# Router logits from unscaled rows with centred gate weights, and the routing's turns, ranks and logits spread over the slots

## The reference, cut

```python
def _ln_t(v, eps=1e-05):
    m = jnp.mean(v, axis=-1, keepdims=True)
    s = jnp.var(v, axis=-1, keepdims=True)
    return (v - m) / jnp.sqrt(s + eps)
...
x = x + _L1_conv_ref(_ln_c(x), ...)              # projections, spikes, attention, output projection
t = _to_tokens(x)
t = t + _L1_ffn_ref(_ln_t(t), ...)
...
def _L1_ffn_ref(x, Wg, bg, W1, b1, W2, b2):
    logits = jnp.einsum('bsd,de->bse', x, Wg) + bg
    topk_vals, topk_idx = jax.lax.top_k(logits, 2)
    topk_w = jax.nn.softmax(topk_vals, axis=-1)
    ...                                          # the two experts of each token, weighted
```

## Time and profile before

| what | us |
|---|---|
| median of 3 runs (1244.0 to 1249.71) | 1247.43 |
| profiled execution | 1248.21 |
| its span | 1246.2 |
| busy: PE / PEld / DVE / ACT / POOL | 980.1 / 822.9 / 828.8 / 625.8 / 550.9 |
| mean granted TensorE clock (share of full speed) | 0.872 |

### The profile page before, as it was taken

One profiled execution on the slowest core, in us unless ns is written; L12 is line 12 of the kernel. 1 busy time (PEld: TensorE's weight loads), 2 busy tenths in 40 slices (PEclk: granted clock), 3 DMA queues, 4 the chain that ended last, 5 costly groups with the idle time before them and its releaser, 6 DMA issues. The chain is left out here.

```text
span 1246.2 us, 23615 instructions
## 1 busy us (share of the span) xinstructions
PE 980.1 (79%) x6627; PEld 822.9 (66%) x6628; DVE 828.8 (67%) x2699; ACT 625.8 (50%) x1334; POOL 550.9 (44%) x707
## 2 busy tenths in 40 slices
PE   9958838767677676876777541499999999999997
PEld 7848825545456464664555530388888888888886
DVE  7724435746759889797885664266666666666665
ACT  3434413475597868778754530244444444444443
POOL 3310001012133566676665764355555554555454
PEclk9979969976778898788877555699999999999999
DMA  8668576900010010000000100111111111111110
GB/s 341 287 186 286 187 212 158 254 19 20 21 51 20 28 46 22 19 26 13 29 15 31 37 25 34 41 51 35 45 48 50 41 48 52 48 41 47 49 40 2
DMA packets 83331, 93.56 MB, mean 75 GB/s; under 512 B 7709, under 2 KB 75549, under 8 KB 79930
## 3 DMA queue, kind: packets, MB, share of 16 engines
q1 hardware_dynamic: 74201, 75.33, 20.5%
q0 software_dynamic: 9056, 17.33, 4.2%
HBM read 56.07 MB, written 38.32 MB: 76 GB/s over the span
## 5 line engine op out<-in xcount | busy, mean ns | idle before, releaser
L1838 POOL DMA_INDIRECT out_dram<-res,index x155 | 154.9, 999 | 216.3 <-DVE res L1904 187.8
L1947 ACT ACTIVATE sil<-ps_h 128x512 f32<-128x512 f32 x155 | 92.6, 597 | 253.0 <-PE ps_h L1999 253.0
L1869 DVE TENSOR_TENSOR act_rows<-ps_h,sil 128x512 f32<-128x512 f32 x155 | 107.2, 692 | 132.3 <-ACT sil L1947 132.3
L2018 PE MATMUL ps_y<-r_raw,aT 128*128 x1240 | 163.8, 275 | 0.0
L159 POOL DMA_INDIRECT slots<-x_sb,r_pos x128 | 129.4, 1011 | 48.3 <-issue 37.3
L2018 PEld LDWEIGHTS ps_y<-r_raw,aT 128*128 128x128 f32 x1240 | 150.7, 192 | 0.1
L1997 PE MATMUL ps_h<-r_raw,uTh 128*128 x310 | 136.6, 441 | 1.6 <-DVE uTl L1863 1.6
L1998 PE MATMUL ps_h<-r_raw,uTh 128*128 x310 | 123.7, 399 | 0.0
L1999 PE MATMUL ps_h<-r_raw,uTl 128*128 x310 | 122.1, 394 | 0.0
L1089 PE MATMUL ps_q<-wqkv,zT 128*128 128x256 f32 x256 | 113.0, 533 | 0.0
L1089 PE MATMUL ps_q<-zT,wqkv 128*128 128x128 f32 x256 | 71.3, 371 | 33.9 <-DVE ps_q L1057 18.3
(11 more groups left out here) (257 smaller groups left out, 2361.9 us busy)
## 6 DMA issues: line engine op xcount, KB each, us to landing
wc<-in_mixing_weights SPq DMA_DIRECT2D x8, 2048.0 KB, 14.8
slots<-zero SPq DMA_DIRECT2D x4, 2652.0 KB, 23.2
pay<-slots SPq DMA_DIRECT2D x39, 272.0 KB, 2.9
x_sb<-in_token_rows SPq DMA_DIRECT2D x8, 1088.0 KB, 6.8
sblk<-coefficients SPq DMA_DIRECT2D x16, 256.0 KB, 6.1
mixed<-mo SPq DMA_DIRECT2D x16, 256.0 KB, 8.2
gin<-mixed SPq DMA_DIRECT2D x16, 256.0 KB, 14.2
r_raw<-in_L_ffn_W SPq DMA_DIRECT2D x8, 508.0 KB
```

The source lines that it names most:

```text
L1838: nc.gpsimd.indirect_dma_start(out_rows, bass.IndirectOffsetOnAxis(at, 0), res[:, m % RES, :], None, bounds_check=TOKENS - 1, oob_is_err=F ...
L1869: nc.vector.tensor_tensor(act_rows[:, k], ps_h[:, k, :, DFF:], sil[:, k], ALU.mult).then_inc(s_act, 1)
L1947: nc.scalar.activation(sil[:, k], ps_h[:, k, :, 0:DFF], ACT.Silu).then_inc(s_sil, 1)
L2018: ins = nc.tensor.matmul(dst, aT[:, k, (2 * e + h) * P:(2 * e + h + 1) * P], raw[:, 4 + h, col], start=(h == 0), stop=(h == 1))
```

## The change

The rows are no longer scaled before the turn. A row's normalised value is (row - mean) times the inverse deviation, so the logits are the inverse deviation times the raw row times gate weights from which the mean over channels is taken off, plus the bias. The centred weights `wg_c` are made once on PE with a matrix `centre` (identity less 1/128). `route_rows` and the buffer `r_y` go; the choice multiplies by the deviation first and so has 16 links.

The order changes with it. On PE a new function `between` stands between `project_out` and `project`: there come the ranks (slot 1 instead of 0), the turns of z in slots 0 to 2, one routing turn in each of slots 3 to 6, and a quarter of the logits in each of slots 4 to 7. On ACT a new function `ahead` stands before the projection's sign: `major`, parts of `u_rows` and `x_rows`, the copies `rT`, and the third group of `z_rows` in slot 7. In pass 0 both kinds stay behind. On DVE the start of the placing moves from slot 0 to 1, its second part from 1 to 2, the deviation from 2 to 3, and two statistics rows stand alone in slot 0. In the tail block 6's turns and logits come in slots 1 and 2, its choice in slot 3, ranks in slot 4, placing in slots 5 and 6; block 7's logits are interleaved with its turns, and the folding of weights comes after block 7's choice.

```diff
         def route_choose(dve, v, rows=None, limit=0):
             dve.wait_ge(s_lg, v + 1)
+            dve.wait_ge(s_rn, v + 1)
             need(dve, s_paid, v)
-            chain.link(nc.vector.tensor_tensor(lg[:, :, :], logits_bank(v).rearrange("p (q e) -> p q e", e=E),
-                                               bg[:, :].unsqueeze(1).broadcast_to([P, NT, E]), ALU.add))
+            by_tile = lambda x: x.rearrange("p (b j) e -> p b j e", j=2)
+            chain.link(nc.vector.tensor_tensor(by_tile(lg[:, :, :]), by_tile(logits_bank(v).rearrange("p (q e) -> p q e", e=E)),
+                                               payload(SCALE, v).unsqueeze(3).broadcast_to([P, B, 2, E]), ALU.mult))
+            chain.link(nc.vector.tensor_tensor(lg[:, :, :], lg[:, :, :], bg[:, :].unsqueeze(1).broadcast_to([P, NT, E]), ALU.add))
...
         def route_turn(pe, v, g):
-            pe.wait_ge(s_ry, v * G + g + 1)
-            if v == NP2 - 1 and g < 2:
+            pe.wait_ge(s_x, (v + 1) * B)
+            if v == NP2 - 2 and g < 2:
                 pe.wait_ge(s_sq, NP2 * B)
+            elif v == NP2 - 1 and g < 2:
+                pe.wait_ge(s_rz, v * G - 2 + g + 1)
...
-        def route_logits(pe, v):
-            pe.wait_ge(s_rz, v * G + 4)
+        def route_logits(pe, v, g0=0, g1=G):
+            pe.wait_ge(s_rz, v * G + g1)
...
             @block.vector, beside(i, b)
-                    if b == 0 and r >= 1:
-                        route_start(dve, r - 1, output_done[r], NT - 2)
+                    if b == 0 and r >= 0:
+                        output_done[r].upto(NT - 2)
+                    if b == 1 and r >= 1:
+                        route_start(dve, r - 1)
                     if b == 1 and r >= 0:
                         route_stats(dve, r, output_done[r])
-                    if b == 1 and r >= 1:
+                    if b == 2 and r >= 1:
                         route_turned_over(dve, r - 1)
-                    if b == 2 and r >= 1:
                         route_place(dve, r - 1)
-                    if b == 2 and r >= 0:
+                    if b == 3 and r >= 0:
                         route_scale(dve, r)
...
+                slot(0)
+                route_stats(dve, w - 1, early)
+                slot(1)
+                route_start(dve, w - 2)
+                route_turned_over(dve, w - 2)
+                route_place(dve, w - 2)
+                slot(2)
+                route_scale(dve, w - 1)
+                slot(3)
+                route_choose(dve, w - 1, late, 6)
+                gap_last(dve, w - 1)
+                slot(4)
+                slot(5)
+                route_start(dve, w - 1)
+                slot(6)
+                route_turned_over(dve, w - 1)
+                route_place(dve, w - 1)
+                slot(7)
+                pay_last(dve, w - 1)
+                late.upto(2 * LAST)
                 add_late(dve, NP2 * B - 1)
-                route_stats(dve, w, output_done[w])
-                route_start(dve, w - 1)
-                route_turned_over(dve, w - 1)
+                route_stats(dve, w, late)
                 route_scale(dve, w)
-                route_place(dve, w - 1)
-                weights_folded(dve)
                 route_choose(dve, w)
                 gap_last(dve, w)
+                weights_folded(dve)
...
             @block.gpsimd, tail
-                scatter(pool, w - 3, 13, NT)
+                pay(pool, w - 2)
                 route_deviation(pool, w - 1)
-                pay(pool, w - 2)
                 scatter(pool, w - 2, 0, NT)
+                scatter(pool, w - 1, 0, 4)
                 route_deviation(pool, w)
-                gap_of(pool, w - 1)
-                pay(pool, w - 1)
-                scatter(pool, w - 1, 0, NT)
+                scatter(pool, w - 1, 4, NT)
                 scatter(pool, w, 0, NT)
...
             @block.scalar
+                def ahead(i, b):
+                    n, r = i + 1, i - 2
+                    if b in (0, 1, 2):
+                        major(act, i, b + 1)
+                    if b == 0 and n < NP2:
+                        u_rows(act, n, 0, 4)
+                    if b == 1 and n < NP2:
+                        u_rows(act, n, 10, 14)
+                    if b == 2 and n < NP2:
+                        x_rows(act, n, 4, 8)
+                    if b in (3, 4, 5, 6) and r >= 0:
+                        route_major(act, r, b - 3)
+                    if b == 3 and n < NP2:
+                        x_rows(act, n, 12, NT)
+                    if b == LAST and n < NP2:
+                        z_rows(act, n, 2)
...
+                        if i:
+                            ahead(i, b)
                         sign_projected(act, i, b)
...
             @block.tensor
+                def between(i, b):
+                    r = i - 2
+                    if b == 1 and r >= 1:
+                        route_rank(pe, r - 1)
+                    if b in (0, 1, 2) and i:
+                        turn(pe, i, b + 1)
+                    if b in (4, 5, 6, 7) and r >= 0:
+                        route_logits(pe, r, b - 4, b - 3)
+                    if b in (3, 4, 5, 6) and r >= 0:
+                        route_turn(pe, r, b - 3)
...
                             project_out(pe, *divmod(k - 1, B))
+                        between(i, b)
                         project(pe, i, b)
...
                     if b == 0:
                         route_rank(pe, w - 2)
+                    if b == 1:
+                        for g in range(G):
+                            route_turn(pe, w - 1, g)
+                    if b in (1, 2):
+                        route_logits(pe, w - 1, 2 * b - 2, 2 * b)
                     if b == 4:
+                        route_rank(pe, w - 1)
...
                 for g in range(G):
                     route_turn(pe, w, g)
-                route_logits(pe, w)
+                    if g:
+                        route_logits(pe, w, g - 1, g)
+                route_logits(pe, w, G - 1, G)
                 route_rank(pe, w)
```

More of the change, by code:

```diff
@@ L1174, in route_turn @@
                 need(pe, s_rz, v * G - 1)
+            elif v < NP2 - 2:
+                pe.wait_ge(s_rz, v * G + g)
             elif g == 1:
@@ L1179, in route_turn @@
             for q in range(G):
-                ins = nc.tensor.transpose(route_bank(v, g)[:, q * P:(q + 1) * P], r_y[:, g * G + q, :], ident[:, :])
+                ins = nc.tensor.transpose(route_bank(v, g)[:, q * P:(q + 1) * P], tile(v)(g * G + q), ident[:, :])
             ins.then_inc(s_rt, 1)
-        def route_logits(pe, v):
-            pe.wait_ge(s_rz, v * G + 4)
+        def route_logits(pe, v, g0=0, g1=G):
+            pe.wait_ge(s_rz, v * G + g1)
+            if v < NP2 - 2 and g0 == 0:
+                need(pe, s_ranked, v)
+            if v == 0:
+                pe.wait_ge(s_centred, 2)
             if v == NP2 - 1:
                 pe.wait_ge(s_kvm, NP2 * 4)
-            for q in range(NT):
-                ins = nc.tensor.matmul(logits_bank(v)[:, q * E:(q + 1) * E], rT[:, q, :], wg[:, :], start=True, stop=True)
-            ins.then_inc(s_lg, 1)
+            for q in range(g0 * G, g1 * G):
+                ins = nc.tensor.matmul(logits_bank(v)[:, q * E:(q + 1) * E], rT[:, q, :], wg_c[:, :], start=True, stop=True)
+            if g1 == G:
+                ins.then_inc(s_lg, 1)
         def route_rank(pe, v):
@@ L1342, in major @@
             nc.scalar.activation(zT[:, g * G:(g + 1) * G, :].rearrange("p q k -> p (q k)"), ps_t[:, 0, :], ACT.Copy).then_inc(s_zT, 1)
[L1344 to L1353, removed]
         def route_major(act, v, g):
             act.wait_ge(s_rt, v * G + g + 1)
-            need(act, s_lg, v)
+            if g == 0:
+                need(act, s_lg, v)
             nc.scalar.activation(rT[:, g * G:(g + 1) * G, :].rearrange("p q k -> p (q k)"), route_bank(v, g), ACT.Copy).then_inc(s_rz, 1)
@@ L1443, in _ @@
                 dve.wait_ge(s_const, 128)
+                nc.vector.tensor_scalar(centre[:, :], ident[:, :], -1.0 / C, None, ALU.add)
                 nc.vector.tensor_copy(before[:, :], before_f[:, :]).then_inc(s_set, 1)
@@ L1456, in _ @@
                 grid_added(dve, 7)
+                dve.wait_ge(s_centred, 1)
+                nc.vector.tensor_copy(wg_c[:, :], ps_log[:, 0:E]).then_inc(s_centred, 1)
                 statistics(dve, 1)
@@ L1502, in _, with slot @@
                 w = NP2 - 1
-                for b in range(B):
+                early, late = output_done[w - 1], output_done[w]
+                def slot(b):
                     if b:
@@ L1550, in beside @@
                     if b >= 3 and r >= 1:
-                        upto_q = (0, 3, 7, 11, 12, 13)
+                        upto_q = (0, 3, 7, 11, 12, 13) if i < NP2 - 1 else (0, 3, 7, 11, 14, NT)
                         scatter(pool, r - 1, upto_q[b - 3], upto_q[b - 2])
@@ L1646, in _ @@
                             spike_output(act, *divmod(k - 1, B))
```

(16 more changed lines are left out.)

74 lines of the change are left out of this document (17 added, 57 removed).

## The result

The changed kernel takes **1256.26 us** (median of 18 runs, 1250.55 to 1263.21), the kernel before 1247.55 beside it (18 runs): ratio 1.0072, 95% interval 1.0056 to 1.0088. It is slower by 8.7 us. I had forecast 1245 in 1235 to 1255, with 0.24 for slower, so the time lies 1.3 us outside the range and on its far side.

The account below looks back on a forecast made before the run. Before the table load at 787.76 us, VectorE's chained work bounds steady passes, chains between engines pass 7 and tail. Terms 0.3 + 8.3 - 3.2 - 7.6 = -2.2 us from 1247.4 gave 1245 us, range 1235 to 1255.

Parts of the forecast that it names:

- The second rival: TensorE becomes the bound in slots 3 to 7; pass 7 loses 5, tail slots 3: 1253 to 1255 us, chance 0.24.
- Part 3: Slots 0 to 3 after a choice: ranks and turn ahead of the projection, placing later; passes 3 to 6 sum +8.3 us.
- Part 2: Slot 7: third group of z rows ahead of the third sign, 1.55 us later in passes 2, 3, 5, 6; pass 4 0.75 sooner.
- slot 7's share: The part of the +8.3 us at pass boundaries carried over from the later choice in slot 7: some 4 us.
- Its sign: Slot 1: VectorE's wait is for the third sign, 2 to 4 us, with the start of the placing behind it.
- Part 4: Pass 7, choice to choice: about 41.0 us where it was 46.75, so -3.5, or -3.2 with its added multiplication.
- Part 5: Tail: 6.0 more up to the last addition, 14.9 less from there to the last choice, +0.3 and +1.0 behind: -7.6 us.
- Links: Multiplication with the deviation adds a step to each of eight choices, 0.33 us each.

Follow-up runs that it names:

- alone it costs 15.0 us: Third group of z rows ahead of the third sign, put alone into the 1226.94 us kernel with everything taken back: 1241.76 us, 0.9963.
- at the higher level: Changed kernel plus 24 unused TensorE products behind the projection in slots 3 to 6 of passes 2 to 6: 1250.36 us, 1.0024.
- Part 3 alone: Ranks and z turns ahead of the projection, placing in slots 1 and 2, ScalarE's rows reordered, put into the 1226.94 us kernel: 1233.25 us, 0.9879.
- all edits taken back: Changed kernel with the steady order of before, and turns and quarters behind the projection in pass 7 too: 1226.94 us, 0.9843.
- that with the turns ahead in passes 2 to 7: Turns and logits quarters alone put ahead of the projection in passes 2 to 7 of the 1226.94 us kernel: 1240.58 us, 0.9951.
- the kernel without the waits: Changed kernel with passes 0 to 6 in the order of before, 1230.84 us; with the 24 unused products added: 1232.39 us, 0.9887.

## Why the prediction was wrong

- **Failed: the cover in slots 4 and 5.** The sum has no term for a quarter and a turn ahead of the projection in steady passes. The second rival gives the reason, "VectorE's own 6 us hides that in steady passes", and Part 3 rests on the same picture, "VectorE doesn't wait in slots 3 to 6". Both took the absence of a wait for room. The room is the 0.51 us between the end of the third sign and VectorE's need of it, since the projection (539.46 to 543.21, at the lower level) already lies under the rows. B: 0 forecast, +7.6 in the trace, 8.9 us in the runs when taken back, 14.1 more when the quarters are doubled, 6.0 less at the higher level. Of the 10.9 us between the forecast of -2.2 and the measured +8.7 this is the largest part. It was the second rival's place, with its price (1.9 us a slot at the slow level) left out of the steady passes. That its 1253 to 1255 came nearest is luck: it put its loss into pass 7 and the tail, which gained 2.4 and 8.1.
- **Right in mechanism: Part 2.** Third sign +1.55 forecast, C +1.53 to +1.68 in the trace in passes 1, 2, 5 and 6 (I had left out pass 1) and +1.09 in pass 3; pass 4, whose C had been 11.53, gained 1.25 (0.75 forecast). Its price was larger than its term: alone it costs 15.0 us, in its trace 9.2 in C and 4.4 in A, where three of four ranks are slow.
- **Part 3: the size by another cause.** Without slot 7's share, my 8.3 us were 4.4 for A of passes 3 to 6; the trace has 3.7. But Part 3 alone gives 0.7 there, with all its ranks at 1.79 us. Its sign came: VectorE's wait in slot 1 of passes 3 to 6 is for the third sign, 2.28 to 3.86 us. Beside Part 3 alone, the changed kernel's slot 1 is 0.3 us longer in pass 3, whose ranks take 1.79, and 1.7 to 1.9 in passes 4 to 6, whose ranks take 2.52 to 3.33. So most of what made A longer goes with the level at which the ranks run. I did take the slow rate of the earlier trace rows, but as given, not as something that Part 2 brings.
- **Part 4: sign right, size too large.** 43.27 us from choice to choice, 41.0 forecast (46.75 to 41.0 with 1.88 is -3.9, where I wrote -3.5). The missing 2.3 lie in slot 4: I allowed at most 5.9 us for a slot, the trace has 8.28 (684.18 less 675.90), with a wait of 5.51 for the third sign behind quarter, turn and projection at the lower level.
- **Right: Part 5.** -7.6 forecast, -8.1 in the trace. VectorE's timeline of the tail in the changed kernel (choice of block 6, last addition, scaling, last choice, folding, start), answering to the earlier trace rows:

```profile
720.44 0.28 DVE L963 TENSOR_TENSOR lg<-ps_turn,x_sb 128x128 f32<-128x128 f32 x1
...
745.96 0.41 DVE L1238 TENSOR_TENSOR x_sb<-x_sb,sy 128x256 f32<-128x256 f32 x1
...
753.02 0.18 DVE L951 COPY x_sb<-r_tmp 128x16 f32<-128x16 f32 x1 [5.01 <-POOL r_tmp L219]
...
756.75 0.29 DVE L963 TENSOR_TENSOR lg<-ps_kv,x_sb 128x128 f32<-128x128 f32 x1 [3.46 <-PE ps_kv L1202]
...
762.32 4.62 DVE L1041 TENSOR_TENSOR r_raw<-r_raw 127x1024 f32<-127x1024 f32 x4
766.86 0.17 DVE L993 TENSOR_TENSOR filled<-fill,ps_turn 128x28 f32<-128x28 f32 x1
```

  Last addition to last choice takes 10.79 us (8 to 11 forecast, 24.3 before), and the power ends 3.7 us ahead of the choice (3 forecast). The slots cost 3.4 rather than 6.0, the turns and logits 1.4 more than taken, choice to start 10.11 where it was 9.00 (+1.3 forecast). That the sum fits so well is in part luck, as the first two errors have opposite signs.
- **Links.** 0.33 each was taken; the choices at the ends of passes 5 and 6 last 6.4 and 6.9 us where they lasted 6.1 and 5.8; the rest wasn't taken apart.
- **Left open.** Pass 0 takes 37.4 or 39.3 us and more, and in some pairs of kernels (all edits taken back, against that with the turns ahead in passes 2 to 7) it differs by 1.9 with the same instructions in that pass. The changed kernel has the longer one, and 1.8 of its 8.2 us are that. What decides it was not tried. Nor was it tried what decides the level of the ranks, or what the tail's parts give one by one.

## What to carry to other kernels

The cover of work moved ahead of a step is not the length of the busy engine's row, but the time from the end of the chain's last instruction to the moment it is wanted, read slot by slot at TensorE's lower level; no recorded wait can mean half a microsecond of room. On an engine that works in order, put what can wait (here next stage's turns and logits) behind the product that a chain waits for, even where the engine idles ahead of it. And look at TensorE's level behind the place that is changed as well as in it: with 1.5 us of sign added, three of the four ranks of passes 3 to 6 took 1.5 us more.

## What the hardware showed that I had not expected

24 products of no use per slot, 1.5 us each time, made the changed kernel faster by 6.0 us: granted clock from slot 3 to z's statistics 1.00 in passes 3 to 6, where it had been 0.67 to 0.87. In the kernel without the waits they gave nothing.

The same sixteen products of the ranks took from 1.79 to 3.38 us, and two edits that don't touch them changed which. The wait ahead of them does not tell: before, 1.33 us stood ahead of 3.38 (pass 6) and 1.89 ahead of 1.79 (pass 4). Part 2 nearly does: in the six kernels here that have it, the changed one among them, 3 of the 24 ranks of passes 3 to 6 took 1.79 or 1.80 us, in the six others without it, before not counted, 19 of 24. Why is open.
